# Indirect transfers of the first FFNs without waits for TensorE's events, in a hybrid of two attentions and two FFNs

## The chip, the cores and the metric

The kernel runs on one core of a Trainium2 chip. TensorE multiplies matrices, VectorE and ScalarE do the elementwise work, GpSimd does some of it and starts the indirect transfers (each moves 128 rows whose addresses come from a list of row numbers), and SyncE (SP) starts the plain loads and stores. Each engine has its own queue of instructions and goes through it in order; the engines meet at semaphores. The metric is the device time of one execution in microseconds, lower is better.

## The reference

The input is x of 4 batches with 1024 tokens of 128 columns. Four blocks follow each other, each normalizes x (layer norm) and adds its result to it:

```python
x = x + _L0_attn_a_ref(_layernorm(x), Wv, ..., b_lk)     # gated attention in groups of 32 tokens
x = x + _L0_ffn_ref(_layernorm(x), Wr, W1, b1, W2, b2)   # experts
x = x + _L0_attn_b_ref(_layernorm(x), q_w, ..., l_b)     # softmax attention, 16 heads of 64
x = x + _L0_ffn_ref(_layernorm(x), Wr, W1, b1, W2, b2)   # the same experts again
```

The change lies in the first FFN block, which runs once for each batch:

```python
probs = jax.nn.softmax(x @ Wr, axis=-1)                  # 8 experts
topk_probs, topk_experts = jax.lax.top_k(probs, K)       # K = 2
...
keep = pos < capacity                                    # 160 slots of each expert and batch
...
buf = buf.at[e_flat, b_idx, pos_c].add(x_rep * keep[..., None].astype(x.dtype))
h = jax.nn.relu(jnp.einsum('ebnc,ech->ebnh', buf, W1) + b1[:, None, None, :])
y = jnp.einsum('ebnh,ehc->ebnc', h, W2) + b2[:, None, None, :]
y_tok = y[e_flat, b_idx, pos_c]
```

Each token chooses two experts, its place within an expert is the count of earlier choices of that expert, and the token's row is written to that slot. The slots go through two layers (128 to 512 to 128 columns), and each token takes back its two answers.

## The kernel before

The order of all work is written by hand, engine by engine, at the end of the kernel (the queues of GpSimd from line 2013, ScalarE 2077, VectorE 2103, TensorE 2140). The batches' attention of the first block runs one after the other on TensorE (`a_tensor`, rows 0 to 3). While one batch is in its attention, the batch before is routed: its normalized tokens are turned and multiplied with the router (`route_turn_tensor`, `logits_tensor`), VectorE chooses the experts (`choose_vector`), TensorE counts the earlier choices (`positions`, a product with a triangle and seven with ones), VectorE turns the counts into places (`kept_vector`), and GpSimd works out the row of each token's slot (`place_gpsimd`, from line 617) into `row_s`. Then GpSimd scatters the batch: 16 indirect transfers (`scatter`, line 666, the call at 670), one for each choice and each tile of 128 tokens, of 512 bytes a row, from the normalized tokens to `xslots` in the chip's memory. The tokens of the first and the third batch lie in `xhat_r` and those of the second in `xhat_r1`, so ScalarE may write the third batch's only when the first batch's scatters are done (`route_norm_scalar`, line 267, by `xhat_scalar`, line 255).

When all attention is done, TensorE runs the FFNs of the first, second and third batch (`experts_tensor`, m = 1, 2, 3; `up_tensor` is the first layer, line 412, and the second is line 446). The fourth batch's FFN comes later, within the softmax attention. SP loads a batch's slots once all its scatters have landed (`load_slots` for the first, line 1990 on for the two others), TensorE turns them (lines 390 and 401), ScalarE copies them out of the accumulators (lines 518 and 524) and adds the bias and the relu behind the first layer (line 542). The answers are turned back (line 470), copied (line 531) and stored, and GpSimd gathers the first batch's answers by 16 indirect transfers (`gather`, line 712).

`hold` (line 165) is a wait with an increment behind it, so that the queue's sequencer stands at the wait before it takes the next instruction. Nearly every scatter has one on an event of TensorE ahead of it: the second batch's, for instance, each stand behind a step of the fourth batch's attention (`scatter_in_attention`: value projection, keys, scores, outputs), the first batch's likewise in the third batch's (`scatter_in_attention`, and `scatter_in_next` for the last three), and the third batch's in pairs behind the first layer of an expert (`beside_expert`, on `f_h`). The gathers stand behind experts in the same way. `f_sc` counts the landed scatters (16 for each), `f_gq` the gathers, `f_idx` the lists of row numbers that are ready, `f_kept` the places from VectorE, and `f_plc` tells that VectorE has worked out the third batch's rows. `bias_gpsimd` adds a bias to a batch's rows for the attention.

## Time and profile before

| | |
|---|---|
| device time, median of 3 runs | 1488.44 us (1484.74 to 1492.68) |
| span of the profiled execution | 1486.9 us |
| TensorE busy (matmuls) | 1437.6 us, 97% |
| TensorE weight loads | 1023.7 us, 69% |
| VectorE busy | 1065.3 us, 72% |
| ScalarE busy | 917.8 us, 62% |
| GpSimd busy | 280.4 us, 19% |
| DMA, mean over the span | 39 GB/s |

The profile is of one execution. Its rows give for each engine what it ran, how long, and in brackets how long it stood idle before and what released it. A releaser "issue" means that the profile shows nothing that was waited for, and "remote" that the end of the wait fits no event that the profile can name. Rows of GpSimd's sequencer (POOLq) show when it passed a wait, which can be before the transfers ahead of it are through. The granted clock is a share of TensorE's full speed: 1.00 is 2.4 GHz, 0.50 is 1.2 GHz.

In time the kernel has these stages: attention of the first block with the routing beside it up to about 137 us, the first three FFNs up to about 214 us, the softmax attention with the fourth batch's FFN and most of the last FFN block, and the last batch's FFN at the end.

### The profile page before, as it was taken

Reading aid. Unit: us, or ns where it says so; the run is one execution under the profiler, and the core shown is the slowest. Engines: PE = TensorE matmul, PEld = TensorE weight load, DVE = VectorE, ACT = ScalarE, POOL = GpSimd, SP = SyncE. Lnnn points to the kernel's source line nnn. Section 1 sums busy time; section 2 is a strip of 40 time slices with the busy share of each in tenths; the row PEclk is TensorE's granted clock in tenths of the full one; section 3 lists DMA queues with packets and bytes.
Section 4 is the critical chain, followed back from the end, with each engine's and each line's share of the span. In section 5 each row is a group of like instructions: output and inputs, shape, how many; then the busy total and the mean of one; then the engine's idle time right before and its main releaser. Section 6 shows DMA issues by size and latency. Waiting matters only on the chain.

```text
span 1486.9 us, 43341 instructions
## 1 busy us (share of the span) xinstructions
PE 1437.6 (97%) x18426; PEld 1023.7 (69%) x18426; DVE 1065.3 (72%) x2172; ACT 917.8 (62%) x1727; POOL 280.4 (19%) x325
## 2 busy tenths in 40 slices
PE   7999789999999999999999999999999999999996
PEld 6988774566677675667777756577777565677486
DVE  6884037888666678886766788876666887787754
ACT  5774466666666666566666666666666666666542
POOL 4164613013210012130000120400001214000055
PEclk9999999999999999999999999999999999999999
DMA  8501221001110011010000110110101101101002
GB/s 223 196 20 53 68 65 39 22 23 46 30 29 16 16 42 32 23 48 16 17 16 16 41 32 22 35 33 17 30 16 39 32 23 34 34 16 30 1 19 58
DMA packets 44464, 58.30 MB, mean 39 GB/s; under 512 B 8231, under 2 KB 32656, under 8 KB 44144
## 3 DMA queue, kind: packets, MB, share of 16 engines
q1 hardware_dynamic: 35120, 38.27, 9.4%
q0 software_dynamic: 9152, 17.26, 4.4%
q8 instruction: 147, 2.41, 0.7%
q14 instruction: 45, 0.37, 0.1%
HBM read 22.14 MB, written 19.32 MB: 28 GB/s over the span
## 4 chain that ended last, share of the span: by engine, by line
PE 87%; DVE 5%; ACT 3%; issue 2%; another core or an unknown queue 2%; DMA 0%; DVEq 0%; ACTq 0%
PE bank L1153 29%; PE bank L1166 28%; PE bank L1076 6%; PE bank L1081 4%; PE bank L1090 4%; PE bank L412 2%; PE bank L446 2%; PE bank L1308 2%; PE bank L1304 2%; DVE nmx L1188 1%; PE bank L1265 1%; ACT hT L542 1%; PE bank L830 1%; DVE stats L1349 1%
## 5 line engine op out<-in xcount | busy, mean ns | idle before, releaser
L1197 ACT ACTIVATE prob<-bank,nmx 128x1024 f32<-128x1024 f32 x512 | 570.2, 1114 | 420.3 <-DVE nmx L1188 408.5
L1188 DVE TENSOR_REDUCE nmx<-bank 128x1 f32<-128x1024 f32 x512 | 626.2, 1223 | 200.2 <-PE bank L1153 182.3
L1166 PE MATMUL bank<-prob,vsc 64*64 64x512 f32 x4096 | 644.9, 590 | 1.9 <-DVE ctxT L1215 1.4
L1153 PE MATMUL bank<-q,k 64*64 64x512 f32 x2048 | 527.6, 591 | 3.1 <-ACT prob L1197 1.9
L1153 PE MATMUL bank<-q,ks 64*64 64x512 f32 x2048 | 526.3, 590 | 0.0
L1166 PEld LDWEIGHTS bank<-prob,vsc 64*64 64x64 f32 x4096 | 237.3, 133 | 119.4 <-issue 47.1
L1076 PE MATMUL bank<-xT,wqkv_sb 64*64 64x256 f32 (+1 forms) x1560 | 211.7, 434 | 0.0
L1153 PEld LDWEIGHTS bank<-q,ks 64*64 64x64 f32 x2048 | 139.1, 133 | 75.9 <-issue 21.0
L1760 POOL DMA_INDIRECT yg<-yslots,row_ring x64 | 64.9, 1014 | 609.2 <-PE bank L1153 579.8
L1153 PEld LDWEIGHTS bank<-q,k 64*64 64x64 f32 x2048 | 135.3, 133 | 37.6 <-issue 8.6
L1076 PEld LDWEIGHTS bank<-xT,wqkv_sb 64*64 64x64 f32 x1560 | 92.2, 133 | 86.6 <-issue 36.5
L1081 PEld LDWEIGHTS bank<-wqkv_sb,xT 64*64 64x64 f32 x1984 | 105.5, 133 | 34.7 <-issue 16.6
L1090 PEld LDWEIGHTS bank<-wl_sb,ctxT 64*64 64x64 f32 x1984 | 108.1, 133 | 28.2 <-issue 8.9
L1081 PE MATMUL bank<-wqkv_sb,xT 64*64 64x128 f32 x1984 | 118.8, 270 | 0.0
L1090 PE MATMUL bank<-wl_sb,ctxT 64*64 64x128 f32 x1984 | 117.4, 270 | 0.3 <-issue 0.3
L1771 POOL DMA_INDIRECT xslots<-xhat_r,row_s x64 | 62.3, 974 | 206.0 <-PE bank L1153 182.7
L1197 ACT ACTIVATION_READ_ACCUMULATOR prob<-bank,nmx 128x1 f32 x512 | 98.7, 193 | 0.0
L1207 DVE TENSOR_TENSOR vsc<-v,zinv 128x128 f32<-128x128 f32 x256 | 74.8, 292 | 8.8
L1132 DVE TENSOR_TENSOR v<-bank,bvv_sb 128x512 f32<-128x512 f32 x64 | 44.2, 691 | 41.5 <-PE bank L1081 41.2
L542 ACT ACTIVATE hT<-bank,b_sb 128x160 f32<-128x160 f32 x160 | 50.0, 411 | 34.7 <-PE bank L412 20.9
L1304 PE MATMUL bank<-xsT,w_sb 64*64 64x160 f32 x768 | 68.2, 296 | 0.0
L1119 DVE TENSOR_TENSOR xres<-bank,xres 128x512 f32<-128x512 f32 x64 | 44.0, 688 | 23.7 <-PE bank L1090 22.0
(270 smaller groups left out, 1628.6 us busy)
## 6 DMA issues: line engine op xcount, KB each, us to landing
ks<-k SPq DMA_DIRECT2D x62, 256.0 KB
yslots<-slots_sb SPq DMA_DIRECT2D x7, 640.0 KB, 3.6
slots_sb<-xslots SPq DMA_DIRECT2D x5, 640.0 KB, 4.5
xslots<-xhat_r POOLq DMA_DIRECT2D x5, 512.0 KB, 7.0
yslots<-xhat_r POOLq DMA_DIRECT2D x5, 512.0 KB, 12.3
w_sb<-in_w SPq DMA_DIRECT2D x1, 2048.0 KB, 9.2
wqkv_sb<-in_wqkv SPq DMA_DIRECT2D x1, 2048.0 KB, 19.0
xslots<-xhat_r,row_s POOLq DMA_INDIRECT x112
```

The costliest lines, as they stand in the source:

```text
L542: ins = nc.scalar.activation(hT[:, e % deep(m), c, :], bank[:, UP_BANK[e % deep(m)] + c // 2, cols(c % 2, CAP)], ACT.Relu, bias=b1_sb[:, e ...
L1076: ins = nc.tensor.matmul(bank[rows(h), PJ[0] + t, 0:n], wqkv_sb[rows(r), row, c + h * HD:c + (h + 1) * HD], xT_c[rows(r), k % 2 * HALF + t ...
L1081: ins = nc.tensor.matmul(bank[rows(h), bk, cols(i)], xT_c[rows(r), cols(8 * (k - 4) + 2 * t + h, HD)], wqkv_sb[rows(r), row, WV:WV + P], s ...
L1090: ins = nc.tensor.matmul(bank[rows(h), bk, cols(i)], ctxT[pi % 2][rows(r), cols(8 * k + 2 * t + h, HD)], wl_sb[rows(r), pi % PAIRS, :], st ...
L1153: ins = nc.tensor.matmul(bank[rows(c), SC[h][n], :], kk[r, cols(2 * j + c, HD)], qst[pi % 2][r, cols(n, HALF)], start=True, stop=True)
L1166: ins = nc.tensor.matmul(bank[rows(h), CX[n], :], vsc[s][rows(r), rows(h)], prob[g % 3][h][rows(r), cols(n, HALF)], start=(j == 0 and firs ...
L1188: nc.vector.tensor_reduce(nmx[:, 2 * s + h:2 * s + h + 1], bank[:, SC[h][0]:SC[h][0] + 2, :], mybir.AxisListType.XY, ALU.max, negate=True) ...
L1197: nc.scalar.activation(prob[g % 3][h][:].rearrange("p (n c) -> p n c", c=HALF), bank[:, SC[h][0]:SC[h][0] + 2, :], ACT.Exp, bias=nmx[:, 2 ...
L1207: nc.vector.tensor_tensor(vsc[s][:].rearrange("p (h c) -> p h c", c=HD), vst[pi % 2][:, j, :].rearrange("p (h c) -> p h c", c=HD), zinv[:, ...
L1304: ins = nc.tensor.matmul(bank[rows(h), bk, cols(q, CAP)], w1_sb[rows(r), e, cols(4 * (i % 2) + 2 * q + h, HD)], xsT[rows(r), cols(e, CAP)] ...
L1760: nc.gpsimd.indirect_dma_start(out=yg[:, k, t, :], out_offset=None, in_=yslots[:, :], in_offset=bass.IndirectOffsetOnAxis(ap=row_ring[:, f ...
L1771: nc.gpsimd.indirect_dma_start(out=xslots[:, :], out_offset=bass.IndirectOffsetOnAxis(ap=row_s[:, k, t:t + 1], axis=0), in_=xhat_r[:, t, : ...
```

## The change

All waits for events of TensorE between the indirect transfers of the first three FFNs go: `scatter_in_attention`, `scatter_in_next` and `beside_expert` are removed (the FFN of the fourth batch isn't touched). GpSimd's order is now: 12 scatters of the first batch, the bias of the fourth row, the second batch's places, the last 4 scatters of the first batch, 16 of the second, a wait for the third batch's rows, 16 of the third, and the 16 gathers. The second batch's row numbers go to a list of their own (`row_s2`), so their place no longer waits for the first batch's scatters. VectorE writes the third batch's row numbers into `row_s` itself, once the first batch's scatters are done, and GpSimd's copy of them and its two waits go. `f_sc` is two semaphores for each batch and `f_gq` two for each quarter, by even and odd transfers, and whoever waits for them waits for both.

On TensorE the count of the third batch's places (`positions`) moves from the middle of the first FFN to ahead of its first expert, and the wait for VectorE's reading of them from the sixth expert's first layer to the third's.

```diff
-        f_sc, f_ld, f_st, f_comb = (sem(n) for n in ("f_sc", "f_ld", "f_st", "f_comb"))
+        f_sc = {m: [sem(f"f_sc{m}{i}") for i in range(2)] for m in (1, 2, 3)}
+        f_ld, f_st, f_comb = (sem(n) for n in ("f_ld", "f_st", "f_comb"))
         f_ga = [sem("f_ga0"), sem("f_ga1")]
-        f_gq = [sem(f"f_gq{q}") for q in range(4)]
...
             elif k == 2:
-                a.wait_ge(f_sc, 256)
+                for done in f_sc[1]:
+                    a.wait_ge(done, 128)
...
+        row_s2 = sb("row_s2", [P, 2, T], U32, stack=stage_f)
...
-                if e == 5 and m == 1:
+                if e == 2 and m == 1:
                     pe.wait_ge(f_kept, 3)
...
 
             def beside(e):
-                if e == 3:
-                    positions(pe, 3, POS_F)
                 if e == E - 1:
-                    pe.wait_ge(f_kept, 3)
                     slots_ahead_tensor(pe, 2, slots2, AHEAD[:2])
...
+        def rows_to(m):
+            return row_s2 if m == 2 else row_s
...
-            if m > 1:
-                p.wait_ge(f_sc, 256 * (m - 1))
-            nc.gpsimd.tensor_copy(row_s[:], skip[:]).then_inc(f_idx, 1)
+            nc.gpsimd.tensor_copy(rows_to(m)[:], skip[:]).then_inc(f_idx, 1)
...
-            nc.vector.tensor_tensor(skip[:], rowf[:], skip[:], ALU.add).then_inc(f_plc, 1)
+            for done in f_sc[1]:
+                v.wait_ge(done, 128)
+            nc.vector.tensor_tensor(rows_to(m)[:], rowf[:], skip[:], ALU.add).then_inc(f_idx, 1)
...
-                v.wait_ge(f_gq[q], 64)
+                for done in f_gq[q]:
+                    v.wait_ge(done, 32)
...
-                nc.gpsimd.indirect_dma_start(out=xslots[:, :], out_offset=bass.IndirectOffsetOnAxis(ap=row_s[:, k, t:t + 1], axis=0),
+                nc.gpsimd.indirect_dma_start(out=xslots[:, :], out_offset=bass.IndirectOffsetOnAxis(ap=rows_to(m)[:, k, t:t + 1], axis=0),
                                              in_=route_rows(m - 1)[:, t, :], in_offset=None,
-                                             bounds_check=B * SLOTS - 1, oob_is_err=False).then_inc(f_sc, 16)
-
-        def scatter_in_attention(p, m, next_row=None):
-
-            r = m + 2
-            hold(p, f_idx, m + 1)
-            hold(p, a_vproj, 4 * r + 4)
-            scatter(p, m, [0])
-            hold(p, a_lktr, 2 * r + 2)
-            scatter(p, m, [1])
...
-        def scatter_in_next(p, m):
-
...
-        def beside_expert(p, i):
-
-            hold(p, f_h, E + i + 1)
+                                             bounds_check=B * SLOTS - 1, oob_is_err=False).then_inc(f_sc[m][c % 2], 16)
+
+        FIRST = 12
 
         def gather(p, step, m, b):
...
                 for k in range(2):
-                    beside_expert(p, 11 + 2 * q + k)
                     for t in (2 * q, 2 * q + 1):
                         nc.gpsimd.indirect_dma_start(out=yg[:, k, t, :], out_offset=None, in_=yslots[:, :],
                                                      in_offset=bass.IndirectOffsetOnAxis(ap=row_g[:, k, t:t + 1], axis=0),
-                                                     bounds_check=B * SLOTS - 1, oob_is_err=False).then_inc(f_gq[q], 16)
+                                                     bounds_check=B * SLOTS - 1, oob_is_err=False).then_inc(f_gq[q][t % 2], 16)
...
         def load_slots(sp, m, b):
             hold(sp, f_st, 16 * m)
-            hold(sp, f_sc, 256 * m)
+            for done in f_sc[m]:
+                hold(sp, done, 128)
...
             for row in range(1, 3):
                 bias_gpsimd(p, row)
             place_gpsimd(p, step, 1)
-            scatter_in_attention(p, 1, 3)
-            scatter_in_next(p, 1)
+            hold(p, f_idx, 2)
+            scatter(p, 1, range(FIRST))
+            bias_gpsimd(p, 3)
             place_gpsimd(p, step, 2)
-            scatter_in_attention(p, 2)
-            scatter(p, 2, [13, 14, 15])
-            p.wait_ge(f_plc, 1)
-            p.wait_ge(f_sc, 256 * 2)
-            nc.gpsimd.tensor_copy(row_s[:], skip[:]).then_inc(f_idx, 1)
+            scatter(p, 1, range(FIRST, 2 * T))
+            hold(p, f_idx, 3)
+            scatter(p, 2, range(2 * T))
             hold(p, f_idx, 4)
-            for i in range(8):
-                beside_expert(p, 3 + i)
-                scatter(p, 3, [2 * i, 2 * i + 1])
+            scatter(p, 3, range(2 * T))
             gather(p, step, 1, 0)
             c_gpsimd(p)
             split_last(p, step)
...
             a_tensor(pe, 3, 2, 1, slots=1)
             pe.wait_ge(load_f, 96)
             pe.wait_ge(f_sub, 4)
+            positions(pe, 3, POS_F)
             experts_tensor(pe, 1, first_batch_tensor(pe), (a_res, 10), following=slots2)
             experts_tensor(pe, 2, second_batch_tensor(pe), begun=True, following=slots3)
             experts_tensor(pe, 3, first_norm_tensor(pe), begun=True)
```

In the fences below, each row is an instruction on one engine with its line, what it writes and reads, and the semaphores it waits for; "x4" means four alike in a row.

GpSimd's queue from the second batch's list of row numbers to the third batch's scatters, before (`row_s` the list, `xhat_r1` the second batch's tokens, the `a_` semaphores and `f_h` events of TensorE):

```order
L635 CAST row_s<-skip 128x16 [waits f_sc,pool_step]
L670 DMA xslots<-xhat_r1,row_s 5120x128 [waits f_idx,a_vproj]
L670 DMA xslots<-xhat_r1,row_s 5120x128 [waits a_lktr]
L670 DMA xslots<-xhat_r1,row_s 5120x128 [waits a_sq]
L670 DMA xslots<-xhat_r1,row_s 5120x128 [waits a_sl] x2
L670 DMA xslots<-xhat_r1,row_s 5120x128 [waits a_kv] x2
L670 DMA xslots<-xhat_r1,row_s 5120x128 [waits a_o] x4
L670 DMA xslots<-xhat_r1,row_s 5120x128 [waits a_out] x2
L670 DMA xslots<-xhat_r1,row_s 5120x128 x3
L2065 CAST row_s<-skip 128x16 [waits f_sc,f_plc]
L670 DMA xslots<-xhat_r,row_s 5120x128 [waits f_idx,f_h]
```

The same stretch after, from the second batch's list to the first gathers:

```order
L635 CAST row_s2<-skip 128x16 [waits pool_step]
L673 DMA xslots<-xhat_r,row_s 5120x128 x4
L673 DMA xslots<-xhat_r1,row_s2 5120x128 [waits f_idx]
L673 DMA xslots<-xhat_r1,row_s2 5120x128 x15
L673 DMA xslots<-xhat_r,row_s 5120x128 [waits f_idx]
L673 DMA xslots<-xhat_r,row_s 5120x128 x15
L681 COPY row_g<-row_ring 128x16 [waits f_comb]
L687 DMA yg<-yslots,row_g 128x128 [waits pool_step,f_st]
L687 DMA yg<-yslots,row_g 128x128 x15
```

The list has its own buffer and stands ahead of the first batch's last four scatters, the thirteen scatters that had waits and the three that had none are one run, and the third batch's 16 and the 16 gathers have one wait each at their head.

TensorE in the middle of the first FFN before: the second layer of the third expert, the count of the third batch's places (`chosen`), and the first layer of the sixth expert (`f_m` is the choice of experts by VectorE, `f_kept` its reading of the counts):

```order
L446 MATMUL bank<-hT,w2_sb 128x160 [waits f_ya,f_ha]
L446 MATMUL bank<-hT,w2_sb 128x160 x3
L379 MATMUL bank<-chosen,before 128x64 [waits f_m]
L381 MATMUL bank<-chosen,ones 128x56
L381 MATMUL bank<-chosen,ones 128x48
L381 MATMUL bank<-chosen,ones 128x40
L381 MATMUL bank<-chosen,ones 128x32
L381 MATMUL bank<-chosen,ones 128x24
L381 MATMUL bank<-chosen,ones 128x16
L381 MATMUL bank<-chosen,ones 128x8
L412 MATMUL bank<-xsT,w1_sb 128x160 [waits f_ha,f_kept]
L412 MATMUL bank<-xsT,w1_sb 128x160 x3
```

TensorE at the end of the fourth batch's attention after: the output projection (`wout_sb`), the count, and the first experts:

```order
L819 MATMUL bank<-wout_sb,gateT 128x128 x15
L381 MATMUL bank<-chosen,before 128x64 [waits f_m,f_sub,load_f]
L383 MATMUL bank<-chosen,ones 128x56
L383 MATMUL bank<-chosen,ones 128x48
L383 MATMUL bank<-chosen,ones 128x40
L383 MATMUL bank<-chosen,ones 128x32
L383 MATMUL bank<-chosen,ones 128x24
L383 MATMUL bank<-chosen,ones 128x16
L383 MATMUL bank<-chosen,ones 128x8
L414 MATMUL bank<-xsT,w1_sb 128x160 [waits f_xs]
L414 MATMUL bank<-xsT,w1_sb 128x160 x3
L414 MATMUL bank<-xsT,w1_sb 128x160 [waits f_xs]
```

The count moved from behind the third expert's second layer to between the attention's output projection and the first expert's first layer, with its wait for the choice of experts.

## Rows read from the trace of the kernel before

**Rows 1.** The page's part 1: busy time of each engine, its share, instructions.

```profile
PE 1437.6 (97%) x18426; PEld 1023.7 (69%) x18426; DVE 1065.3 (72%) x2172; ACT 917.8 (62%) x1727; POOL 280.4 (19%) x325
```

**Rows 2.** Stretches: length, busy us (PE, PEld, DVE, ACT, POOL), clock, DMA, GB/s.

```profile
37.00:74.00 37.00, 36.62 (x285) 34.75 (x286) 31.98 (x120) 26.39 (x48) 6.07 (x6) 1.00 0.59 198
...
130.00:135.00 5.00, 5.00 (x25) 5.00 (x25) 3.78 (x17) 1.73 (x4) 0.49 (x1) 0.50 0.05 14
```

**Rows 3.** Waits, 112 to 205 us: engine, tile, line, releaser; sum, times, longest.

```profile
ACT hT L542 <- remote: 9.7, 3, 3.7
```

**Rows 4.** Timeline: start, duration, work; in brackets the wait before it and its releaser.

```profile
126.20 1.08 ACT L331 ACTIVATE xT_r<-bank 128x512 f32<-128x512 f32 x2 [6.33 <-remote]
...
198.52 1.25 PE L412 MATMUL bank<-xsT,w_sb 128*128 128x160 f32 x8
...
202.59 1.25 ACT L542 ACTIVATE hT<-bank,b_sb 128x160 f32<-128x160 f32 x4 [3.43 <-remote]
```

**Rows 5.** GpSimd's sequencer, line 168 in three windows: passed waits (ns; first, last start).

```profile
L168 POOLq EVENT_SEMAPHORE  x1: 17/17/17, 119.0 to 119.0; - x1
...
L168 POOLq EVENT_SEMAPHORE  x2: 17/17/17, 126.1 to 126.7; - x2
...
L168 POOLq EVENT_SEMAPHORE  x1: 17/17/17, 197.6 to 197.6; - x1
```

**Rows 6.** Timeline, TensorE in the attention of the third and fourth batch.

```profile
90.30 0.61 PE L830 MATMUL bank<-attnT,vact 128*128 128x128 f32 x4
...
93.64 1.04 PE L313 MATMUL bank<-ident,xhat 128*128 128x128 f32 x8
...
94.52 1.85 PE L370 MATMUL bank<-wr_sb,xT_r 128*128 128x8 f32 x16
...
99.80 0.47 PE L767 MATMUL bank<-xT_hi,wa_hi 128*128 128x512 f32 x1
...
121.11 0.61 PE L830 MATMUL bank<-attnT,vact 128*128 128x128 f32 x4
...
137.18 3.42 PE L412 MATMUL bank<-xsT,w_sb 128*128 128x160 f32 x24
```

**Rows 7.** Timeline, TensorE between the FFNs.

```profile
154.38 1.04 PE L401 MATMUL bank<-ident,vact 128*128 128x128 f32 x8
...
167.16 1.35 PE L412 MATMUL bank<-xsT,w_sb 128*128 128x160 f32 x8 [1.07 <-ACT slots_sb L531]
...
181.95 1.04 PE L401 MATMUL bank<-ident,state 128*128 128x128 f32 x8
...
194.13 1.26 PE L470 MATMUL bank<-ident,yT 128*128 128x128 f32 x10
...
196.24 1.35 PE L412 MATMUL bank<-xsT,w_sb 128*128 128x160 f32 x8 [0.86 <-ACT slots_sb L531]
...
199.60 1.25 PE L446 MATMUL bank<-hT,w_sb 128*128 128x160 f32 x8
```

**Rows 8.** GpSimd: line 670 grouped (ns min, median, max), then timeline.

```profile
L670 POOL DMA_INDIRECT xslots<-xhat_r,row_s x48: 966/975/1625, 79.9 to 171.4; - x48
...
108.95 0.33 POOL L620 TENSOR_TENSOR rowmat<-tmp,rowbase 128x64 f32<-128x64 f32 x1
...
114.66 1.03 POOL L670 DMA_INDIRECT xslots<-xhat_r,row_s  x1 [0.95 <-POOL row_s L635]
...
115.99 1.02 POOL L670 DMA_INDIRECT xslots<-xhat_r,row_s  x1 [0.30 <-issue]
...
1428.65 1.34 POOL L1820 DMA_INDIRECT owners<-owner,row_s  x1 [8.53 <-DVE row_s L1845]
```

**Rows 9.** Timeline: VectorE's counts, ScalarE's overwriting, ScalarE late in the kernel.

```profile
103.66 0.21 DVE L615 TENSOR_SCALAR tmp<-bank 128x64 f32<-128x64 f32 x1
...
116.68 3.19 ACT L255 ACTIVATE xhat_r<-xres,shift,rstd 128x128 f32<-128x128 f32 x8 [2.16 <-issue]
...
1441.52 1.36 ACT L518 ACTIVATE xsT<-bank 128x512 f32<-128x512 f32 x3 [7.92 <-issue]
```

More of the change, by code:

```diff
@@ L132, in bass_hybrid @@
         f_kept = sem("f_kept")
-        f_plc = sem("f_plc")
         f_xs, f_ha, f_ya, f_ys = (sem(n) for n in ("f_xs", "f_ha", "f_ya", "f_ys"))
-        f_sc, f_ld, f_st, f_comb = (sem(n) for n in ("f_sc", "f_ld", "f_st", "f_comb"))
+        f_sc = {m: [sem(f"f_sc{m}{i}") for i in range(2)] for m in (1, 2, 3)}
+        f_ld, f_st, f_comb = (sem(n) for n in ("f_ld", "f_st", "f_comb"))
         f_ga = [sem("f_ga0"), sem("f_ga1")]
-        f_gq = [sem(f"f_gq{q}") for q in range(4)]
+        f_gq = [[sem(f"f_gq{q}{i}") for i in range(2)] for q in range(4)]
         f_gb = [sem("f_gb0"), sem("f_gb1")]
@@ L1415, in f_norm_vector @@
                 else:
-                    v.wait_ge(f_sc, 256 * (B - 1))
+                    for done in f_sc[B - 1]:
+                        v.wait_ge(done, 128)
                 xhat_vector(v, c0, fb, xhat_r, piece - 5, g_xhat)
@@ L1992, in _ @@
                     store_slots(sp, 1, 0)
-                hold(sp, f_sc, 256 * m)
+                for done in f_sc[m]:
+                    hold(sp, done, 128)
                 hold(sp, f_ld, 16 * m)
```

22 lines of the change are left out of this document (removed).

## The prediction

> **What bounds the kernel now.** I read the page first: TensorE is busy 97% of the span [rows 1], so a change on GpSimd's queue can only pay where TensorE stands still or runs at its lower clock. Then the table of stretches: in the stretch that the change touches, the attention of the third and fourth batch and the first FFNs, the granted clock falls to 0.50 (1.2 GHz) in 130 to 135 us, after TensorE had stood still between its products [rows 2]. Then the waits of 112 to 205 us. ScalarE's first FFN layer waits 9.7 us for a releaser that the profile can't name ("remote") [rows 3], and so, in the timeline, does its copy of the turned tokens, for 6.33 us [rows 4]. Each of them waits for a TensorE event by the code.
>
> The timeline shows what these waits are: TensorE's work is done, and its event arrives late. The up product of 198.52 us takes 1.25 us, and ScalarE starts on it at 202.59 us, after 3.43 us of waiting [rows 4]. I looked where this happens. GpSimd was then in a run of indirect transfers without a gap, each time at least some 5 us old, and the late events came when the run had ended. GpSimd's sequencer, which runs ahead of its transfers, passes a wait at 119.0 us, stands at the next one, for an attention output of TensorE, and passes that at 126.1 us [rows 5]; ScalarE, waiting for another event of TensorE, goes on at 126.20 us [rows 4]. So one blockage holds the events for both engines. What feeds it is what this prediction turns on: that GpSimd's queue holds waits for TensorE's events between its transfers, or the runs of transfers as such.
>
> **The removed waits.** Three losses, each measured against the same work undisturbed.
>
> Attention of the fourth batch, from the second half of its value products to the first expert product: 121.11 to 137.18 us, 16.07 us [rows 6]. The third batch took 90.30 to 99.80, 9.50 us, with the turn of the next batch in it (93.64 to 94.52, 0.88 us for eight 128-column transposes, 0.11 each), which the fourth doesn't have; the fourth turns ten tiles of slots instead (1.10). Undisturbed it would take 9.50 - 0.88 + 1.10 = 9.72 us. Loss 6.35 us, the lower clock included.
>
> From the first to the second FFN: from the first transposes of the next slots (154.38) to the third up product (167.16), 12.78 us [rows 7]. Undisturbed: eight transposes 0.88, one product of an expert 1.08 (198.52 to 199.60 [rows 4, 7]), two transposes 0.22, two up products 2.16, and turning the answers back with ScalarE's copies 2.11 (194.13 to 196.24, not held up). Sum 6.45. Loss 6.33 us. From the second to the third FFN: 181.95 to 196.24, 14.29 us, loss 7.84 us. Smaller waits inside the FFNs (below 0.5 us each) I leave out.
>
> Together 20.5 us, if TensorE's events arrive in time everywhere.
>
> **What is late next.** GpSimd now issues 12 scatters of the first batch in one run, adds a bias, places the second batch, and then issues 4 + 16, 16, and 16 gathers. One scatter takes 0.975 us (median) [rows 8], and 0.30 us lie between two, so about 1.28 us each. The place of the second batch started at 108.95, behind the last scatter, though VectorE's counts were ready at 103.66 + 0.21 [rows 8, 9]. It now starts there, some 5 us earlier; from its start to the first scatter it takes 114.66 - 108.95 = 5.71 us [rows 8]. So the last four scatters of the first batch start at about 109.6 and have landed at about 116 (an estimate: four by 1.28, and about 1.3 to land, as between the last scatter and the load). ScalarE overwrites what they read at 116.68 [rows 9]: 0.7 us to spare, and each microsecond beyond that delays TensorE's next turn. The 16 of the second batch then end near 135, their load near 141, and TensorE asks for them at about 148 (154.38 - 6.35). The third batch's scatters end near 157, its gathers of answers near 180, and the norm that waits for these is some 2 us ahead of TensorE's transposes. All of that is hidden; the thinnest cover is the 0.7 us.
>
> The positions of the third batch's tokens move on TensorE from between the experts to ahead of them. Their own matmuls (below 0.5 us) stay; the wait for VectorE's counts inside the FFN goes (0.45 us, not in the sum); a wait for the choice of experts comes. VectorE's chain from the logits to the choice takes about as long as TensorE's slots and output projection in between, so I put this edit between -0.4 and +0.5 us, at nothing. VectorE now writes the row numbers itself, and GpSimd's copy and its two waits go; SP's loads wait for two counts instead of one. Both come earlier than their users need them.
>
> New in the queue are waits behind runs of transfers for events of ScalarE (the bias) and VectorE (the third place). If such a wait holds up events of these engines until the run ends, as TensorE's are held up now, it costs at most about 2 us once, as the run of 12 ends near 95.5 and TensorE would turn the next batch at 93.64 [rows 6]; the nearest row without cost is the same bias at present, so 0 to 2 us. For this and for ScalarE's copies between the FFNs (0 to 0.5 us twice) I take 1.5 us. Net gain 19 us. The span is 1486.9 us and the median of the runs 1488.44, 1.5 us above it; 1488.44 - 19 is **1469 us**, with 1463 to 1477 as this case's own range: the upper end if the lower clock stays in places or a third of the losses does.
>
> **The rivals.** For the forecast speaks that the events of TensorE alone are late, and GpSimd waits for TensorE; that heavy traffic doesn't do it, for in 37 to 74 us the DMA engines are busy 59% at 198 GB/s while TensorE works 36.62 of 37 us [rows 2]; and a run of twelve indirect transfers near the end, from 1428.65 us [rows 8], which has no wait in between: 13 us into it ScalarE starts at 1441.52 [rows 9] on what TensorE has just finished.
>
> *First rival, slower: the run itself blocks the events.* Against the forecast speaks that at 198.52 to 202.59 us GpSimd's sequencer had passed its last wait for TensorE at 197.6 [rows 5] and stood at one for VectorE, and still the event was late; and the twelve transfers of the end move 8 bytes a row where these move 512. If the age of a run decides, then runs older than 5 us cost. Before there are runs of 8, 10, 6, 10 and 6 transfers, at 1.28 us: together 26 us beyond the first 5 us of each, and 20.5 us lost, 0.79 us for one. After, runs of 12, 20, 16 and 16 give 62 us, 49 us lost: 28 us slower at worst. The run of 12 lies beside attention with few waiters, so I take 20 us: 1508 us. It decides from 20.5/62, that is if one microsecond of a long run costs more than 0.33 us.
>
> *Second: only part of the losses goes*, because some events still wait for runs that are now longer: gain and loss cancel, 1481 to 1496 us.
>
> *Third: scatters slow beside VectorE.* The 20 scatters move beside VectorE's attention work. By the slowest one [rows 8], 1.63 + 0.30 us, they would take 39 us and not 26; the load would end near 154, TensorE would wait 6 us for it, and the time would be 1475 us. On this the Trainium skill's page "SBUF — State Buffer", section "Who interferes with whom", says that VectorE and GpSimd share a pair of ports by an exclusive lock, and the page's section on the bandwidth pool gives about 3.1 us for a transfer of GpSimd that takes 0.62 us alone. By that rule a run of 20 would take some 60 us (an estimate) and the kernel would be slower by more than 10 us. The trace speaks against it: 975 ns is the median and 966 the least of 48 scatters, of which two thirds lie beside attention.
>
> *Fourth: it doesn't do what it says*: the last gathers and the whole second half keep their waits, which is as the change means it; here nothing more is at stake.
>
> **How the numbers follow.** Forecast 0.54, third rival 0.04: both faster by more than 0.5% (below 1481 us; half a percent, 7.4 us, is about what a measurement of this kernel can tell from no change), with 0.02 more from the faster edge of the second rival. Second rival 0.11, of which 0.09 within 0.5%. First rival 0.31, slower. That gives 0.60, 0.09 and 0.31. The range must reach into the slower case: 1462 to 1507 leaves out half of the first rival and a little below, about 0.2. The forecast's own range is 1463 to 1477.
>
> **What would show it.** Right: no wait of ScalarE or VectorE for an unnamed releaser between 110 and 200 us; a clock of 1.00 there; GpSimd's transfers in runs of 12, 20, 16 and 16; the fourth batch's stretch near 9.7 us and the two gaps between FFNs near 6.5 us each; the second half of the kernel about 19 us earlier and otherwise unchanged. Wrong: events of TensorE that arrive at the end of these runs, the more the longer the run, and TensorE idle in the fourth batch's attention from about 5 us after the run of 20 begins. If ScalarE's write of the normalized tokens (116.68 now) starts more than 1 us later against its neighbours, the four late scatters cost.

## The result: 1523 us, slower by 2.3%

The changed kernel takes 1523.23 us (median of 4 runs, 1521.18 to 1524.50), the kernel before 1490.11 us beside it. The ratio is 1.0229, with a 95% interval of 1.0209 to 1.0249: slower by 33 us. The forecast was 1469 us with a range of 1462 to 1507, so the time lies outside it, on the side of the first rival, and above that rival's own 1508.

The profiled execution has a span of 1520.6 us, 33.7 us more than before. The page's part 1 of the changed kernel, to set beside [rows 1]: the instructions are the same but for one of GpSimd's, TensorE's share falls, and its products take 8.9 us longer in sum.

```profile
PE 1446.5 (95%) x18426; PEld 1028.5 (68%) x18426; DVE 1065.7 (70%) x2172; ACT 918.7 (60%) x1727; POOL 280.9 (18%) x324
```

The table of stretches of the changed kernel (columns as in [rows 2]) shows where TensorE stands still. In each of these 5 us it is busy for 0.5 to 3.0 us; its granted clock is 0.74 in the first of them and 0.50 (1.2 GHz) in the others:

```profile
130.00:135.00 5.00, 3.04 (x12) 2.05 (x12) 0.42 (x1) 0.00 (x0) 3.79 (x4) 0.74 0.06 13
140.00:145.00 5.00, 1.58 (x5) 1.02 (x4) 0.69 (x1) 0.00 (x0) 2.92 (x3) 0.50 0.06 14
175.00:180.00 5.00, 1.12 (x4) 1.15 (x5) 0.00 (x0) 0.39 (x1) 3.85 (x4) 0.50 0.12 39
...
220.00:225.00 5.00, 0.54 (x2) 0.57 (x3) 1.42 (x6) 1.08 (x3) 1.24 (x2) 0.50 0.14 31
```

The late events that were to go are there, and longer. The timeline of the changed kernel, ScalarE and VectorE (start, duration, work, and in brackets the wait before it and its releaser):

```profile
97.65 1.08 ACT L332 ACTIVATE xT_r<-bank 128x512 f32<-128x512 f32 x2 [5.57 <-remote]
...
142.49 0.69 DVE L940 TENSOR_TENSOR gateT<-bank,gateT 128x512 f32<-128x512 f32 x1 [11.62 <-remote]
...
146.86 1.08 ACT L332 ACTIVATE xT_r<-bank 128x512 f32<-128x512 f32 x2 [19.42 <-remote]
...
184.06 1.28 ACT L541 ACTIVATE hT<-bank,b_sb 128x160 f32<-128x160 f32 x4 [5.32 <-remote]
```

The copy of the turned tokens, which waited 6.33 us in [rows 4], now waits 19.42 us. It goes on 3.2 us after GpSimd's run of 20 scatters is over. That run starts at 118.16 us, and its last transfer ends at 142.66 + 0.97 = 143.63 us:

```profile
118.16 1.02 POOL L673 DMA_INDIRECT xslots<-xhat_r,row_s  x1 [0.52 <-issue]
...
142.66 0.97 POOL L673 DMA_INDIRECT xslots<-xhat_r,row_s  x1 [0.30 <-issue]
```

TensorE's own rows give the account by stages. First the marks of the changed kernel that answer to [rows 6], with the first product of the softmax attention as the last one, and three rows from inside the run of 20:

```profile
90.22 0.61 PE L797 MATMUL bank<-attnT,vact 128*128 128x128 f32 x4
...
107.50 0.48 PE L734 MATMUL bank<-xT_hi,wa_hi 128*128 128x512 f32 x1
...
124.40 0.61 PE L797 MATMUL bank<-attnT,vact 128*128 128x128 f32 x4
...
133.98 0.27 PE L314 MATMUL bank<-ident,xhat_r 128*128 128x128 f32 x1 [1.09 <-issue]
134.70 0.27 PE L314 MATMUL bank<-ident,xhat_r 128*128 128x128 f32 x1 [0.45 <-issue]
135.40 0.27 PE L314 MATMUL bank<-ident,xhat_r 128*128 128x128 f32 x1 [0.43 <-issue]
...
157.05 1.20 PE L414 MATMUL bank<-xsT,w_sb 128*128 128x160 f32 x7
...
249.30 1.94 PE L1015 MATMUL bank<-xT,wqkv_sb 128*64 128x512 f32 x8
```

In the kernel before the softmax attention began at 214.01 us:

```profile
214.01 2.37 PE L1048 MATMUL bank<-xT,wqkv_sb 128*64 128x512 f32 x10
```

| stretch on TensorE | before | after | difference |
|---|---|---|---|
| third batch's second half of values to the fourth's projections | 9.50 | 17.28 | +7.78 |
| from there to the fourth's second half of values | 21.31 | 16.90 | -4.41 |
| from there to the first expert | 16.07 | 32.65 | +16.58 |
| the three FFNs, to the softmax attention | 76.83 | 92.25 | +15.42 |
| sum | 123.71 | 159.08 | +35.37 |

Behind that, 1.6 us are made good up to the end. The four runs of transfers end in the three stretches that lose: 12 in the first, 20 in the third, 16 and 16 in the FFNs. Even single transposes, which wait for nothing new, come 0.7 us apart in the run of 20: not only TensorE's events are slow there, TensorE is too. So the wait of 19.42 us has two parts: the last of the eight transposes ends at 135.40 + 0.27 = 135.67 us, and from there ScalarE still waits 11.2 us for the event.

### The profile page after: what moved, and what is told of

It is laid out like the page before. It is cut to its first block, busy times and chain, and to the rows that moved or that the text cites. A ratio compares the mean times of both kernels' runs of the same rounds, so it can differ in the third digit from the quotient of the medians.

```text
span 1520.6 us, 43302 instructions
## 1 busy us (share of the span) xinstructions
PE 1446.5 (95%) x18426; PEld 1028.5 (68%) x18426; DVE 1065.7 (70%) x2172; ACT 918.7 (60%) x1727; POOL 280.9 (18%) x324
## 4 chain that ended last, share of the span: by engine, by line
PE 86%; DVE 7%; issue 3%; ACT 2%; another core or an unknown queue 2%; DMA 0%; DVEq 0%; ACTq 0%
PE bank L1120 28%; PE bank L1133 28%; PE bank L1043 6%; PE bank L1057 4%; PE bank L1048 4%; PE bank L1275 2%; PE bank L1271 2%; PE bank L414 2%; PE bank L448 2%; DVE nmx L1155 2%; PE bank L797 1%; PE bank L1232 1%; PE bank L801 1%; PE bank L789 1%
## 5 line engine op out<-in xcount | busy, mean ns | idle before, releaser
L448 PE MATMUL bank<-hT,w_sb 128*128 128x160 f32 x320 | 55.5, 321 | 23.8 <-ACT yT L547 13.7
## 6 DMA issues: line engine op xcount, KB each, us to landing
wqkv_sb<-in_wqkv SPq DMA_DIRECT2D x1, 2048.0 KB, 19.2
```

The costliest lines, as they stand in the source:

```text
L448: ins = nc.tensor.matmul(bank[:, 6 + e % 2, 0:CAP], w2_sb[:, e, c, :], hT[:, e % deep(m), c, :], start=(c == 0), stop=(c == HC - 1))
```

## The experiments

The question left by the result: what in a run of transfers holds TensorE up? All sixteen kernels below ran beside the kernel before; the ratios are to it. "Transfers" are the 64 indirect ones of the first three FFNs. This table gathers all but the last. The pace is the mean distance between the starts of sixteen scatters, from the first one after 113 us on. They are the second batch's, or, where 12 scatters come first, the last four of the first batch and twelve of the second. Pauses and waits between them are counted in: the runs of the kernel before, of fours and of eights go at 1.28 us. The unnamed waits are all those of ScalarE and VectorE between 75 and 240 us that end "remote", added up. Small delays keep a name and are not in the sum.

| kernel | pace, us | unnamed waits, us (longest) | ratio (95% interval) |
|---|---|---|---|
| before | 1.83 | 33 (6.3) | 1 |
| changed | 1.29 | 75 (19.4) | 1.0229 (1.0209 to 1.0249) |
| two ahead | 1.69 | 1.5 (1.2) | 1.0085 (1.0045 to 1.0125) |
| fours | 1.69 | 0.8 (0.8) | 1.0044 (1.0018 to 1.0071) |
| narrow | 1.31 | 78 (18.3) | 1.0263 (1.0233 to 1.0293) |
| four ahead | 1.30 | 72 (19.2) | 1.0256 (1.0235 to 1.0277) |
| four ahead, bias early | 1.32 | 62 (18.9) | 1.0227 (1.0208 to 1.0245) |
| eights | 1.50 | 39 (8.8) | 1.0083 (1.0063 to 1.0104) |
| two ahead and waits | 1.74 | 0 | 1.0082 (1.0058 to 1.0106) |
| two ahead, 16 first | 1.76 | 0 | 1.0002 (0.9988 to 1.0015) |
| every fourth | 1.45 | 31 (5.2) | 1.0028 (1.0012 to 1.0044) |
| small work | 1.32 | 59 (13.0) | 1.0189 (1.0161 to 1.0217) |
| long work | 1.62 | 0 | 0.9954 (0.9940 to 0.9969) |
| short work | 1.49 | 16 (2.6) | 1.0007 (0.9995 to 1.0018) |
| before, paced | 1.63 | 0 | 0.9984 (0.9972 to 0.9996) |
| changed, paced | 1.62 | 0 | 1.0004 (0.9991 to 1.0018) |
| middle work | 1.56 | 0 | 0.9942 (0.9919 to 0.9965) |

### Age, backlog or bytes

Two ahead holds each transfer until the one two places before it has landed:

```diff
+        def landed(p, m, c):
+            c = c - 2
+            if c < 0 and m > 1:
+                m, c = m - 1, c + 2 * T
+            if c >= 0:
+                hold(p, f_sc[m][c % 2], 16 * (c // 2 + 1))
...
             for c in tiles:
                 k, t = c // T, c % T
+                landed(p, m, c)
```

> The changed kernel, with each of its 64 indirect transfers of the first FFNs held until the one two places before it has landed, so that GpSimd's sequencer is never more than two transfers ahead. A transfer lands about 2.2 us after its start and the one two places on starts 2.56 us after it, so GpSimd should still run them back to back (about 1.3 us apart, runs of 20, 16 and 16). Theory A (the age of a run of transfers stops TensorE's events, from some 5 us on): the time stays at that of the changed kernel, 1515 to 1528 us. Theory B (transfers that the sequencer has pushed ahead of GpSimd stop them): 1463 to 1480 us, with no wait for an unnamed releaser over 2 us in 75 to 215 us. Theory C (only waits for TensorE in GpSimd's queue, the forecast) is the forecast that failed and would give no difference to the changed kernel.

1497.47 us, between both ranges. In the trace no unnamed wait is longer than 1.2 us, as the theory of the backlog has it. The time that stays has other reasons. TensorE waits 6.5 us for the third batch's slots and 11.8 us for the norm behind the gathers, since 64 transfers at this pace end later. And GpSimd's bias now lies beside VectorE's choice of experts, where one comparison of 0.23 us takes 2.78 us (two ahead, VectorE and GpSimd):

```profile
101.91 2.78 DVE L590 TENSOR_TENSOR eq<-pr,ptop 128x64 f32<-128x64 f32 x1
...
102.17 2.43 POOL L295 TENSOR_TENSOR xres<-xres,bout_sb 128x1024 f32<-128x1024 f32 x1
```

The Trainium skill's page "SBUF — State Buffer", section "SBUF: two separate sides", says that an instruction of VectorE with two inputs in that memory and one of GpSimd that reads it exclude each other for a whole instruction. These rows agree: VectorE's ends at 104.69 us, GpSimd's at 104.60. That section also says that the one that starts first goes through. This the rows don't show, for VectorE's starts 0.26 us earlier and is the one held up.

Fours pushes four transfers at once and then waits until all have landed:

```diff
+            elif c % BURST == 0 and c:
+                for done in f_sc[m]:
+                    hold(p, done, 8 * c)
```

> The changed kernel, with its indirect transfers in fours: four are pushed at once, and the next four wait until all have landed, which makes runs of about 5.1 us and pauses of about 1.8 us. Theory A (age of a run, reset by a pause) and theory B (backlog, at most four here) both expect most of the loss to go: 1463 to 1490 us, the later end because 20 transfers then take about 35 us and the second batch's slots arrive some microseconds late. If pauses of this size don't reset what blocks TensorE, it stays above 1505 us.

1492.80 us, and no unnamed wait over 0.8 us: a run of four with a pause of 2 us behind it does no harm. The slots come late here too (8.3 us).

Narrow writes 8 bytes a row into a spare table, in place of 512 into the slots (which stay unfilled):

```diff
-                ... out=xslots[:, :], ... in_=route_rows(m - 1)[:, t, :]
+                ... out=owners[:, :], ... in_=route_rows(m - 1)[:, t, 0:2]
```

> The changed kernel, with its 48 scatters writing 8 bytes of each row into a spare table instead of 512 bytes into the slots (the experts then work on zeros; same count of transfers, of rows and of waits). Theories A and B, by count and time of transfers: 1510 to 1526 us. Theory C2 (the bytes moved decide, as the run of 8-byte rows near the end of the kernel suggests): the losses of the scatters go and only the gathers' stay, 1475 to 1495 us.

1526.07 us, as slow as the changed kernel: bytes are not it. Age and backlog were still both possible, since two ahead had left gaps.

### Four ahead against the backlog, eights, and the waits

Four ahead is two ahead with a distance of four and four counters a batch; bias early moves the bias behind the eighth scatter.

```diff
+                hold(p, f_sc[m][c % 4], 16 * (c // 4 + 1))
...
-            scatter(p, 1, range(FIRST))
+            scatter(p, 1, range(8))
             bias_gpsimd(p, 3)
+            scatter(p, 1, range(8, FIRST))
```

> The changed kernel with each indirect transfer of the first FFNs held until the one four places before it has landed (four counters a batch instead of two), so that the sequencer is at most four ahead and GpSimd runs back to back at 1.28 us. Theory B (backlog): no late events, and since 20 transfers now take 26 us and not the 35 to 39 us of two ahead and of fours, the slots arrive in time; what is left is the bias of the fourth row, which stands beside VectorE's choice of experts and held it for 2.5 us with two ahead. 1470 to 1482 us. Theory A (age of a run at full pace; with two ahead the gaps were 0.3 to 1 us): late events from 6 us into the runs, above 1500 us.

> As four ahead, with the bias of the fourth row behind eight scatters of the first batch instead of twelve, where VectorE waits for TensorE. Theory B: 2 to 4 us below four ahead, 1466 to 1478 us, faster than both kernels. Theory A: above 1500 us.

1524.17 and 1519.93 us. The theory of the backlog falls: with at most four ahead, as in fours, the events are as late as in the changed kernel. What differs is that GpSimd runs without a gap (four ahead, GpSimd and ScalarE):

```profile
126.19 0.97 POOL L692 DMA_INDIRECT xslots<-xhat_r,row_s  x1 [0.30 <-issue]
127.47 0.97 POOL L692 DMA_INDIRECT xslots<-xhat_r,row_s  x1 [0.30 <-issue]
...
148.02 1.09 ACT L332 ACTIVATE xT_r<-bank 128x512 f32<-128x512 f32 x2 [19.25 <-remote]
```

Two ahead had left a gap of 0.7 to 1 us ahead of every second transfer (two ahead, GpSimd):

```profile
130.01 0.97 POOL L692 DMA_INDIRECT xslots<-xhat_r,row_s  x1 [0.30 <-issue]
131.83 0.97 POOL L692 DMA_INDIRECT xslots<-xhat_r,row_s  x1 [0.84 <-issue]
133.10 0.97 POOL L692 DMA_INDIRECT xslots<-xhat_r,row_s  x1 [0.31 <-issue]
135.04 0.97 POOL L692 DMA_INDIRECT xslots<-xhat_r,row_s  x1 [0.96 <-issue]
```

Eights is fours with `BURST = 8`.

> The changed kernel with its transfers in eights: eight are pushed at once, the next eight wait until all have landed. Theory B with a limit between four and eight: events of TensorE are late again in each eight, by 2 to 5 us, 1490 to 1512 us. If the limit lies above eight: no wait for an unnamed releaser above 2 us, and 1470 to 1490 us.

1498.47 us, with unnamed waits of up to 8.8 us: a run of eight at 1.28 us is long enough to do harm, although the pauses bring the mean to 1.50.

Two ahead and waits puts the waits for TensorE back ahead of the third batch's pairs and of the gathers:

```diff
-            scatter(p, 3, range(2 * T))
+            for i in range(8):
+                hold(p, f_h, E + 3 + i + 1)
+                scatter(p, 3, [2 * i, 2 * i + 1])
```

> Two ahead, with the waits for TensorE's first layer put back ahead of each pair of the third batch's scatters and of the gathers, as before the change. If waits for TensorE in GpSimd's queue hold up its events by themselves (the forecast's reason): waits for an unnamed releaser of 2 us and more return in 150 to 215 us and the time grows by 5 to 15 us over the 1497 us of two ahead. If only the backlog does it: no such waits, and 1492 to 1503 us.

1498.35 us and not one unnamed wait. The waits ahead of the third batch's scatters and of the gathers hold up nothing by themselves, and there the forecast's reason falls. Those of the first two batches come back in a later run (before, paced).

### An idle engine, or the pace

From here on the first batch's 16 scatters stand in one run, with the bias behind eight of them and ahead of the second batch's places. Two ahead, 16 first is two ahead in that order; every fourth keeps only the wait ahead of each fourth transfer; small work has no such waits, but clears one column of a spare tile ahead of every second transfer.

```diff
+            scatter(p, 1, range(8))
             bias_gpsimd(p, 3)
+            scatter(p, 1, range(8, 2 * T))
             place_gpsimd(p, step, 2)
-            scatter(p, 1, range(FIRST, 2 * T))
...
+                if c % 4 == 0:
+                    landed(p, m, c)
...
+                if c % 2 == 0:
+                    nc.gpsimd.memset(breath[:, ...], 0.0)
```

> Two ahead, with all 16 scatters of the first batch ahead of the second batch's places (GpSimd stood idle there) and the bias of the fourth row behind eight of them, out of the way of VectorE's choice. Theory D, formed after eights and four ahead: TensorE's events stop when GpSimd runs transfers with no more than 0.30 us between them for over some 5 us, however many are queued; gaps of 0.7 us and more, as two ahead leaves in every second or third place, let them through. It expects no late events and the second batch's slots some 4 us earlier: 1478 to 1494 us. Theory B (backlog) expects the same here.

> The order of the run before, but only every fourth transfer waits, for the landing of the one two places before it: four back to back, then a gap of 0.6 to 1 us, about 1.4 us for a transfer. Theory D: if such a gap ends the blockage for four transfers, no late event above 2 us, 1470 to 1484 us, below both kernels. If after four transfers a gap as in fours (2 us) is needed: late events as in eights, 1495 to 1515 us. Theory B: at most six ahead, between fours and eights, 1480 to 1500 us.

> The same order without waits for landings; ahead of every second transfer GpSimd clears one column of a spare tile, a work of some 0.1 to 0.2 us, so that it does something else in between without standing idle. If the idle engine is what lets the events through (theory D): as the changed kernel, 1508 to 1528 us. If any other instruction between two transfers does: no late events, 1468 to 1486 us.

1488.98, 1494.42 and 1517.75 us. Two ahead, 16 first has no unnamed wait, as both theories expected. In every fourth the gaps are there, and events still wait 5 us for the next one (every fourth, VectorE and GpSimd):

```profile
131.69 0.69 DVE L962 TENSOR_TENSOR gateT<-bank,gateT 128x512 f32<-128x512 f32 x1 [5.17 <-remote]
...
134.15 0.98 POOL L693 DMA_INDIRECT xslots<-xhat_r,row_s  x1 [0.82 <-issue]
...
137.43 0.69 DVE L962 TENSOR_TENSOR gateT<-bank,gateT 128x512 f32<-128x512 f32 x1 [5.04 <-remote]
```

So a gap of 0.8 us after two transfers is enough, and after four it isn't: that fits a mean pace with a limit better than a pause of a given length that resets something. The small work of 0.12 us disappears in the 0.30 us between transfers and leaves most starts 1.28 us apart, so it told the two apart less well than meant. The next two runs do: they slow the pace while GpSimd is kept busy.

```diff
+        def work(step):
+            step.wait()
+            step.done(nc.gpsimd.tensor_tensor(idle_sb[:], idle_sb[:], idle_sb[:], ALU.add))
...
             for c in tiles:
                 k, t = c // T, c % T
+                work(step)
```

The spare tile `idle_sb` has 128 columns in long work and 48 in short work.

> The order of the last three runs; no waits for landings, but ahead of each transfer GpSimd adds a spare tile of 128 columns to itself (about 0.4 us by the adds of its own places), so that it is never idle and yet starts a transfer only every 1.5 to 1.65 us. Theory E, formed after the last runs: each transfer keeps something busy for about 1.45 us, TensorE's events pass only when that is free, and at 1.28 us a transfer it is never free again after some 5 us, until the run ends (the release came 1.4, 1.9, 2.5 and 3.2 us after the end of runs of 8, 12, 16 and 20). Theory E: no late event above 2 us, slots and answers earlier than with two ahead, 1468 to 1486 us. Theory D (GpSimd must stand idle): late events as in the changed kernel, 1505 to 1530 us.

> The same with a spare tile of 48 columns (0.2 to 0.3 us), a transfer every 1.38 to 1.5 us. Theory E: near its limit; below about 1.42 us a transfer, late events return and it is slower than the run with the long work, 1485 to 1515 us; if the pace comes out at 1.45 us or more, none and 1466 to 1484 us. Theory D: late events, 1505 to 1530 us.

Long work: 1481.11 us, half a percent faster than before, and no unnamed wait at all, though within its runs GpSimd stands idle for no more than 0.17 us between two instructions (long work, GpSimd and ScalarE; this copy waited 19.42 us in the changed kernel):

```profile
119.94 0.99 POOL L682 DMA_INDIRECT xslots<-xhat_r,row_s  x1 [0.17 <-issue]
120.95 0.41 POOL L675 TENSOR_TENSOR idle_sb<-idle_sb 128x128 f32<-128x128 f32 x1
121.53 1.00 POOL L682 DMA_INDIRECT xslots<-xhat_r,row_s  x1 [0.16 <-issue]
122.56 0.42 POOL L675 TENSOR_TENSOR idle_sb<-idle_sb 128x128 f32<-128x128 f32 x1
...
121.50 1.09 ACT L332 ACTIVATE xT_r<-bank 128x512 f32<-128x512 f32 x2 [0.76 <-PE bank L314]
```

Short work, at 1.46 us from start to start (1.49 in the mean), has fourteen unnamed waits, none above 2.6 us, and 1489.87 us. It is slower than its lower branch had allowed at that pace: the limit lies higher than I put it. Its rows also show how the late events get through (short work, TensorE, GpSimd and ScalarE):

```profile
128.67 1.40 PE L393 MATMUL bank<-ident,slots_sb 128*128 128x128 f32 x10
...
133.64 1.00 POOL L682 DMA_INDIRECT xslots<-xhat_r,row_s  x1 [0.17 <-issue]
133.97 0.60 ACT L518 ACTIVATE xsT<-bank 128x512 f32<-128x512 f32 x1
135.10 0.99 POOL L682 DMA_INDIRECT xslots<-xhat_r,row_s  x1 [0.17 <-issue]
135.42 0.60 ACT L518 ACTIVATE xsT<-bank 128x512 f32<-128x512 f32 x1 [0.85 <-remote]
136.57 0.99 POOL L682 DMA_INDIRECT xslots<-xhat_r,row_s  x1 [0.17 <-issue]
136.87 0.39 ACT L518 ACTIVATE xsT<-bank 128x256 f32<-128x256 f32 x1 [0.85 <-remote]
```

TensorE has turned all ten tiles of slots by 130.07 us. ScalarE's three copies of them start at 133.97 us (behind other late work), 135.42 and 136.87, each 0.3 us after a transfer's start. The events have piled up and pass here one a transfer. The theory that the engine must stand idle falls; the pace it is.

### The same on both kernels, and the last stage

Before, paced is the kernel before with all its waits and the add of 128 columns ahead of each transfer. Changed, paced is the changed kernel with that add alone. Middle work is long work with 96 columns.

> The kernel before with all its waits for TensorE, and the spare add of 128 columns ahead of each of the 64 transfers (one every 1.6 us or slower). Theory E (the pace of the transfers): the late events of 112 to 205 us go here too, 1468 to 1482 us against 1488. If waits for TensorE in the queue are a cause by themselves: waits for an unnamed releaser of 2 us and more stay, 1485 to 1500 us.

> The changed kernel in its own order with the spare add of 128 columns ahead of each transfer, and nothing else. Theory E: no late event above 2 us; the bias in front of the second batch's places and beside VectorE's choice costs 2 to 5 us over the run with the long work (1481): 1480 to 1490 us. If the other order was what helped: above 1500 us.

> As the run with the long work (1481 us), with a spare tile of 96 columns: a transfer every 1.53 to 1.57 us. Theory E with a limit below that: no late event above 1 us and, as 48 transfers end about 2.5 us earlier, 1476 to 1482 us. If the limit lies between 1.55 and 1.60 us: late events of 0.5 to 2 us as with the short work, 1481 to 1489 us.

1483.62 us (a little above what was expected), 1487.14 and 1477.21 us, and no unnamed wait in any of them. The pace alone takes 1523 back to 1487 us in the changed kernel, and it clears the kernel before with all its waits in place, though that one's time falls by 0.2% only: its slower transfers let TensorE wait 5.5 us for the third batch's slots and 4.5 us for the norm behind the gathers. In this stage the limit is thus between 1.49 us (some late) and 1.56 us (none), in the mean. Middle work has the lowest ratio of the table, 0.9942 of the kernel before. What it still waits for is the gathers: the norm behind them comes 6.31 us late for TensorE (middle work, TensorE):

```profile
199.99 2.05 PE L498 MATMUL bank<-ident,xhat 128*128 128x128 f32 x8 [6.31 <-DVE xhat L1351]
...
204.10 2.39 PE L1025 MATMUL bank<-xT,wqkv_sb 128*64 128x512 f32 x8
```

The last run (tail paced) adds the same work at the end of the kernel, to the last batch's 16 gathers and to the last four transfers of the owners' table, which tells the token of each slot:

```diff
+                    if b == B:
+                        work_last(step)
                     nc.gpsimd.indirect_dma_start(out=yg[:, k, t, :], ...
```

> The run with the spare tile of 96 columns (1477 us), and the same add ahead of the last four transfers of the owners' table and of the 16 gathers of the last batch, which run at 1.28 to 1.31 us in the kernel before with two late events (2.5 us, and 9.7 us beside other work, after which TensorE stands idle 2.7 and 2.5 us). Theory E holds there too: no late event above 1 us in the last 40 us, TensorE's two idle stretches shorter by 3 to 5 us together, 1472 to 1477 us. If the last stage's late events have another cause (its waits for TensorE, say): they stay and the slower gathers cost, 1477 to 1483 us.

1480.22 us, a ratio of 0.9942 (0.9926 to 0.9958), as without it. The late events of that stage go (ScalarE's longest unnamed wait there, 9.7 us before and 8.64 in middle work, becomes 6.62 us, for a named product), so the pace holds up events there too; the time doesn't follow, because the slower gathers now end last and VectorE waits for them (tail paced, ScalarE and VectorE):

```profile
1461.69 0.88 ACT L1857 ACTIVATE answers<-bank,slot_owner 128x128 fp32r<-128x128 f32 x3 [6.62 <-PE bank L1877]
...
1475.57 1.14 DVE L1454 SCALAR_TENSOR_TENSOR xres<-yg,wtok_ring,xres 128x128 f32<-128x128 f32 x4 [3.55 <-DMA yg<-yslots,row_ring]
```

## Why the prediction was wrong

**What bounds the kernel, and the size of the losses: right.** The late events of TensorE were what could be won, and the undisturbed times were sized well. Middle work shows them (TensorE; the second halves of values, the first expert, the next slots and the third up products):

```profile
123.28 0.61 PE L807 MATMUL bank<-attnT,vact 128*128 128x128 f32 x4
133.60 1.60 PE L415 MATMUL bank<-xsT,w_sb 128*128 128x160 f32 x10
149.98 1.04 PE L404 MATMUL bank<-ident,vact 128*128 128x128 f32 x8
...
156.39 1.35 PE L415 MATMUL bank<-xsT,w_sb 128*128 128x160 f32 x8 [0.80 <-ACT slots_sb L531]
...
171.69 1.06 PE L404 MATMUL bank<-ident,state 128*128 128x128 f32 x8 [0.91 <-DMA state<-xslots]
...
178.19 1.35 PE L415 MATMUL bank<-xsT,w_sb 128*128 128x160 f32 x8 [0.86 <-ACT slots_sb L531]
```

The fourth batch's stretch is 10.32 us (9.72 foretold), the two gaps between FFNs are 6.41 and 6.50 us (6.45 foretold).

**The cause: wrong, and this is the step that failed.** "What feeds it is what this prediction turns on", and it chose the waits for TensorE over the runs. The runs showed the opposite: with such waits in place and a slower pace no wait is unnamed (before, paced), and without any of them, back to back, 75 us of waits are (changed). Waits and runs always stood together in the kernel before, so nothing in that trace could part them. The one row that did speak to it, the sequencer past its last such wait at 197.6 us with the event still late [rows 5], was named as evidence for the rival and then given too little weight. And the two rows that spoke against the rival were not alike. The traffic of 37 to 74 us holds no run of indirect transfers. The run of twelve at the end was taken for the same thing with smaller rows; its first nine go at 1.40 us and not at 1.28, and TensorE's events are few there (GpSimd, and ScalarE's second wait in that stretch):

```profile
1430.30 1.06 POOL L1820 DMA_INDIRECT owners<-owner,row_s  x1 [0.31 <-issue]
...
1440.08 0.98 POOL L1820 DMA_INDIRECT owners<-owner,row_s  x1 [0.30 <-issue]
...
1444.06 1.25 ACT L542 ACTIVATE hT<-bank,b_sb 128x160 f32<-128x160 f32 x4 [1.17 <-PE bank L412]
```

From 1430.30 to 1440.08 us that is seven transfers in 9.78 us. The distance alone doesn't explain why nothing was late: in every fourth (1.45) and short work (1.49) events were. But TensorE ran from 1432.61 us through one chain of products that told ScalarE nothing before 1441.5, so no events could pile up as they do in short work. That this is the difference is argued; no run tests it. The row was thus no proof against the rival, and it stays a row that the pace alone doesn't account for.

**The first rival: right in its mechanism, too small in its term.** Of the 28 us that its price gave it took 20, because the run of 12 "lies beside attention with few waiters". That run cost the third batch's stretch 7.78 us. With all four runs counted, 62 us beyond the first 5 us cost about 20.5 + 35.4 = 56 us, or 0.90 us each and not 0.79: 35 us more than before. The price also left out a run of seven at 79.94 to 88.98 us, after which nothing waited unnamed; with it the sum gives 0.68 us each and 22 us.

**What is late next: overtaken.** The second batch's places start at 111.63 us and not 5 us before 108.95, since TensorE itself is late. The cover of 0.7 us is gone (ScalarE waits 2.2 us for the four late scatters), but beside the rest it doesn't show. The positions cost TensorE no wait in the changed kernel and 0.2 us in middle work, at nothing as was said. The scatters don't slow beside VectorE (median 972 ns), so the third rival didn't happen.

**Why not 1469 even without late events.** The sum let the transfers run at 1.28 us. That pace is what can't be had: at 1.54 us from start to start the 64 transfers take 17 us more, and of the 19.9 us that middle work wins in the three stretches it gives 6.3 back to the gathers. Its softmax attention begins at 204.10 us, 9.9 us earlier than before, in a profile that started 2.2 us late (see the end).

## What to carry to other kernels

A long run of indirect transfers from GpSimd can hold up TensorE and those that wait for it, although the transfers themselves take no longer than usual (0.97 us): look at the distance between their starts, and if events of TensorE arrive together when the run ends, slow the run (here from 1.28 to 1.54 us) rather than take waits away. Waits that seem to block can be what paces a queue; before removing them, ask what will then run back to back. And a counterexample counts only when its rows have the same distance, length and neighbours as the case; here the neighbours were events of TensorE that could pile up.

## What was not expected of the hardware

- TensorE's events, and its own instructions, are held up by the pace of indirect transfers: from some 5 us into a run at 1.28 us, with waits of up to 19.4 us, and with rows of 512 and of 8 bytes alike. At 1.49 us the waits are 2.6 us at most, at 1.56 us there are none. The run of twelve at the end, at 1.40 us and with few events, stays unexplained.
- Only TensorE's events are late. The trace also holds the times at which semaphores were updated. From 75 to 215 us the updates of ScalarE, VectorE and GpSimd come within 0.02 us of the end of their instruction, in every run. TensorE's come up to 15 us behind it in the changed kernel, but at most 0.04 us behind it in long work, in middle work and in the two kernels of the table that are called paced.
- The release follows the end of a run by more, the longer it was: 1.5 us after the run of 8 (before), 2.0 after 12, 2.7 after 16 scatters, 2.4 after 16 gathers and 3.2 after 20 (changed). That is 0.15 to 0.19 us a transfer, as if each kept something busy for about 1.45 us that TensorE needs free. This picture is argued from these numbers, not shown; the limit that was measured, above 1.49 us, lies higher, and what that something is stays open; the first late event also came at different ages (between 5 and 10 us).
- The profiles fall into two kinds of start, 2.2 us apart before any of these transfers begins (the second batch's first product of values and keys stands at 52.03 us before, 52.35 in the changed kernel and 51.87 in long work, but at 54.28 in two ahead and within 0.5 us of that in all others). No run tells why.
